# Four layers on one core, attention: the bf16 parts of q and k are made and read back one attention step further ahead

## The reference

```
x = layernorm(x + mamba(x))        # selective scan, 256 channels, 16 states
x = layernorm(x + ffn_fp4(x))      # gate/up/down with blockwise fp4 of x, h and the weights
x = layernorm(x + attention(x))    # the layer that the change touches
x = layernorm(x + mlp(x))          # 128 -> 512 -> 512 -> 128 with weights +1/-1
```

```
q, k = rope(x Wq), rope(x Wk)                    # per map, 8 dimensions
o1   = softmax(q1 k1^T * 8**-0.25) v             # v has 16 columns per head
o2   = softmax(q2 k2^T * 8**-0.25) v
o    = rms_norm(o1 - lam * o2) * ln_w + ln_b ;   out = (o * (1 - 0.8 + 0.6 exp(-3.6))) Wo
```

## Time and profile before

| | us |
|---|---|
| median of 3 runs | 1071.04 |
| lowest and highest run | 1065.42, 1078.87 |
| the profiled execution's own time | 1068.53 |
| its span, first to last instruction | 1066.7 |

### The profile page before, as it was taken

The page is one execution under the profiler, slowest core; times in us unless marked ns, Lnnn a source line. Parts: engine busy times, 40 slices in busy tenths (PEclk is TensorE's granted clock), DMA queues, the critical chain, the costliest instruction groups (busy, mean ns, idle before and its releaser), DMA issues.

```text
span 1066.7 us, 14636 instructions
## 1 busy us (share of the span) xinstructions
PE 912.0 (85%) x4466; PEld 481.7 (45%) x4482; DVE 891.7 (84%) x1337; ACT 731.5 (69%) x1600; POOL 788.1 (74%) x560
## 2 busy tenths in 40 slices
PE   7697979897989797786888679999999898699995
PEld 3233434342434343233556454565655543355453
DVE  4799999999999999998885667787777783479996
ACT  3776868686868686544565457777777768777872
POOL 2798998989898989875777734575756535767773
PEclk9899999899999999899999889999999999899998
DMA  4762535353434434003400323332323210000001
GB/s 149 318 239 79 205 113 200 118 199 119 177 142 152 166 141 177 0 1 81 66 0 16 104 76 90 92 99 83 99 83 102 80 47 2 0 2 12 18 21 30
DMA packets 35168, 104.03 MB, mean 98 GB/s; under 512 B 3659, under 2 KB 22475, under 8 KB 24395
## 3 DMA queue, kind: packets, MB, share of 16 engines
q1 hardware_dynamic: 35095, 103.16, 28.9%
HBM read 93.84 MB, written 8.91 MB: 96 GB/s over the span
## 4 chain that ended last, share of the span: by engine, by line
DVE 28%; PE 26%; issue 17%; ACT 15%; DMA 7%; POOL 4%; SPq 4%; DVEq 1%; POOLq 0%; ACTq 0%
PE bank L1644 11%; DVE bank L333 8%; PE bank L610 8%; DMA ks<-parts 6%; PE bank L2002 4%; DVE m_hC L342 4%; DVE a_nm L1410 3%; ACT bank L461 2%; DVE m_hS L333 2%; ACT L461 2%; SPq L1362 1%; DVE m_du L347 1%; SPq L1373 1%; DVE x_all L122 1%; DVE bank L914 1%
## 5 line engine op out<-in xcount | busy, mean ns | idle before, releaser
L610 PE MATMUL bank<-m_hC,ident 128*128 128x512 f32 x512 | 257.8, 627 | 61.4 <-POOL m_hC L568 22.7
L558 POOL TENSOR_TENSOR m_dBu<-m_du,m_Bt 128x1024 f32<-128x1024 f32 x128 | 299.3, 2356 | 12.6 <-DMA m_Bt<-bcd 11.8
L333 DVE TENSOR_TENSOR_SCAN bank<-bank,m_dBu 128x512 f32<-128x512 f32 x184 | 222.4, 1219 | 16.5 <-ACT bank L461 12.6
L1410 DVE TENSOR_REDUCE a_nm<-bank 128x2 f32<-128x512 f32 x256 | 169.3, 687 | 66.7 <-PE bank L1644 66.5
L1581 ACT ACTIVATE late<-bank 128x512 f32<-128x512 f32 x256 | 148.9, 600 | 65.2 <-PE bank L1644 63.4
L610 PEld LDWEIGHTS bank<-m_hC,ident 128*128 128x128 f32 x512 | 93.9, 196 | 203.9 <-issue 111.5
L461 ACT ACTIVATE bank<-m_delta,early 128x510 f32<-128x510 f32 x256 | 170.0, 677 | 0.3
L1644 PE MATMUL bank<-ks,qs 72*128 72x256 bf16 x512 | 100.4, 279 | 28.7 <-DMA ks<-parts 16.8
L342 DVE TENSOR_TENSOR m_hC<-bank,m_Ct 128x512 f32<-128x512 f32 x184 | 123.3, 670 | 0.0
L568 POOL TENSOR_TENSOR m_hC<-m_hS,m_Ct 128x512 f32<-128x512 f32 x72 | 94.6, 1315 | 26.6 <-DVE m_hS L333 26.6
L458 ACT ACTIVATE bank<-m_zero 128x2 f32<-128x2 f32 x181 | 31.2, 173 | 115.5 <-DVE m_hC L342 114.9
(11 more groups left out here) (217 smaller groups left out, 1797.1 us busy)
## 6 DMA issues: line engine op xcount, KB each, us to landing
m_Bt<-bcd SPq DMA_DIRECT2D x32, 1024.0 KB, 6.3
m_Ct<-bcd SPq DMA_DIRECT2D x32, 1024.0 KB, 6.6
qs<-parts SPq DMA_DIRECT2D x16, 576.0 KB
ks<-parts SPq DMA_DIRECT2D x48, 192.0 KB
parts<-a_part SPq DMA_DIRECT2D x32, 192.0 KB, 2.2
out<-x_all SPq DMA_DIRECT2D x8, 256.0 KB, 2.3
vx<-in_vrow SPq DMA_DIRECT2D x4, 256.0 KB
qs<-in_fill SPq DMA_DIRECT2D x1, 768.0 KB
```

Source lines behind the costliest of these rows:

```text
L333: nc.vector.tensor_tensor_scan(out, decay, dBu[:, g % RD], 0.0, ALU.mult, ALU.add).then_inc(scan_ready, 1)
L558: nc.gpsimd.tensor_tensor(dBu[:, g % RD:g % RD + CH], du[:, n % 2], Bt[:, s].unsqueeze(1).broadcast_to([P, CH, GTOK]), ALU.mult).then_inc( ...
L610: return nc.tensor.matmul(out, lhsT, rhs, start=start, stop=stop)
L1410: nc.vector.tensor_reduce(nm[:, slot % 2, q, 2 * pair:2 * pair + 2], s1[i % 2][:], AX.X, ALU.max, negate=True).then_inc(max_ready, 1)
```

## The change

Everything that was done for item n + 3 in step n's first slots is now done for item n + 4 in step n's last slots, so each item is ready earlier.

- GpSimd: `rotate(n+4)` stays at u = 7 (10 in the lone steps). `normalize(n-3)` moves from u = 0 to u = 8. `residual_high(n+4)` stands at u = 9 (lone: 13), `copy_x(n+5)` at u = 10 (lone: 6), `residual_middle(n+4)` at u = 11 (lone: 15). The wait for the transposes of x moves from `residual_middle` to `copy_x`. `head_norm` stays at u = 14.
- ScalarE: the cast to the high part moves from u = 15 to u = 12, the cast to the middle part from u = 4 of the next step to u = 15 of the same.
- SyncE: in a step the three rows go out first, then the parts of item n + 4 are written and read back, into the slot that item n still uses; the read waits until the scores of item n are done (`s2_ready`).

No instruction is added or taken away.

```diff
     def sync(sp):
         def body(n, slot):
-            m, s = n + 3, (slot + 3) % RING
-            if has(n, 3):
-                sp.wait_ge(split_p, 2 * m + 2)
-                for i in range(2):
-                    sp.dma_start(k.parts[i].rearrange("a p t -> p a t"), part[:, :, i, :]).then_inc(parts_out, 16)
             if has(n, 1):
                 sp.wait_ge(nmT_ready, n + 2)
...
-            if has(n, 3):
+            if has(n, 4):
+                m = n + 4
+                sp.wait_ge(split_p, 2 * m + 2)
+                for i in range(2):
+                    sp.dma_start(k.parts[i].rearrange("a p t -> p a t"), part[:, :, i, :]).then_inc(parts_out, 16)
                 sp.wait_ge(parts_out, 32 * m + 32)
+
+                wait(sp, s2_ready, MAPS * (n + 1))
...
-                sp.dma_start(qs[0:ROWS, s].rearrange("r m t -> r (m t)"),
+                sp.dma_start(qs[0:ROWS, slot].rearrange("r m t -> r (m t)"),
...
-                    sp.dma_start(ks[24 * a:24 * a + 24, s].rearrange("r m t -> r (m t)"), k3).then_inc(q_in, 16)
+                    sp.dma_start(ks[24 * a:24 * a + 24, slot].rearrange("r m t -> r (m t)"), k3).then_inc(q_in, 16)
...
             wait(pool, q_in, 64 * m)
-            wait(pool, x_turned, min_group(m + 2, BATCH))
             nc.gpsimd.tensor_tensor(part[:, 2].rearrange("p a t -> p (a t)"), res[:],
...
             for u in range(MAPS):
-                if u == 0 and has(n, 3):
-                    residual_high(n + 3)
-                if u == 0 and has(n, -3):
+                if u == (6 if lone(n) else 10) and has(n, 5):
+                    wait(pool, x_turned, n + 5)
+                    copy_x(n + 5)
+                if u == (10 if lone(n) else 7) and has(n, 4):
+                    rotate(n + 4)
+                if u == (8 if has(n, 4) else 0) and has(n, -3):
                     normalize(n - 3)
-                if u == 5 and has(n, 3):
-                    residual_middle(n + 3)
-                if u == 6 and has(n, 5):
-                    if not has(n, 3):
-                        wait(pool, x_turned, n + 5)
-                    copy_x(n + 5)
-                if u == 7 and has(n, 4):
-                    rotate(n + 4)
+                if u == (13 if lone(n) else 9) and has(n, 4):
+                    residual_high(n + 4)
+                if u == (15 if lone(n) else 11) and has(n, 4):
+                    residual_middle(n + 4)
                 if u == 14 and has(n, -1):
                     head_norm(n - 1)
...
-                if u == 4 and has(n, 3):
-                    act.wait_ge(split_p, 2 * (n + 3) + 1)
-                    nc.scalar.activation(part[:, 1].rearrange("p a t -> p (a t)"), res[:], ACT.Copy).then_inc(split_a, 1)
...
-                if u == 15 and has(n, -2):
-                    squares(n - 2)
-                if u == 15 and has(n, 4):
+                if u == 12 and has(n, 4):
                     m = n + 4
                     act.wait_ge(rope, 2 * m + 2)
                     wait(act, parts_out, 32 * m)
                     wait(act, split_p, 2 * m)
                     nc.scalar.activation(part[:, 0], rot[:], ACT.Copy).then_inc(split_a, 1)
+                if u == 15 and has(n, -2):
+                    squares(n - 2)
+                if u == 15 and has(n, 4):
+                    act.wait_ge(split_p, 2 * (n + 4) + 1)
+                    nc.scalar.activation(part[:, 1].rearrange("p a t -> p (a t)"), res[:], ACT.Copy).then_inc(split_a, 1)
                 yield
```

## The result

| | before | after |
|---|---|---|
| median of 6 runs each, us | 1071.88 (1065.42 to 1078.87) | 1058.26 (1057.07 to 1059.37) |
| ratio, 95% interval | | 0.987 (0.984 to 0.990) |
| the profiled execution, us | 1068.53 | 1057.07 |
| its span, us | 1066.7 | 1055.2 |

The kernel is 1.3% faster: 13.6 us in the medians, 11.5 us between the two profiled executions, against 16.2 forecast for the latter. The median lies inside the stated range of 1044 to 1064. TensorE is busy for 915 us, 912 before, so the time came out of waits (first row: the page's part 1, which answers to the earlier trace rows; then TensorE's waits: line, releaser, us in total, times, longest).

A forecast was written before the change was run, and what follows sets the result against it. Attention was taken as bound by TensorE's own list, a too-late read and something on VectorE; -11.5 (ten steps), -2.0 (step 12), -4.2 (early steps) and +1.5 (VectorE contact) gave -16.2 us, from 1068.5 to 1052, range 1044 to 1064.

The forecast's parts named there:

- The read in the middle: Steps 1 to 11: parts read lands 6 us before it is wanted, its waits go, -11.5 us over ten steps.
- The contact on VectorE: head_norm beside VectorE's five short instructions: only its last row holds a cast, 0.15 us a step, +1.5 us in all.
- rival 1: GpSimd's head_norm takes over the hold of VectorE in every step: 8.5 us back, 1060 us; chance 0.13.
- ScalarE's second cast: ScalarE's cast to the middle part, before slot 0's exponential: starts 0.8 us after its input, so costs nothing.
- rival 4: ScalarE held at the second cast by a late input: 15 steps grow, 1078 us at 2.5 us late; chance 0.07.
- the sign named for it: ScalarE waiting on GpSimd's `a_res` in front of L1630 would speak for rival 4.
- The small rows: Three rows sent at 8.0 us, queued behind the read: land about 14.5, wanted at 15.9, hidden with 1.4 us cover.
- Step 12 and the tail: Step 12 loses its 1.94 us wait for the read: -2.0 us with the small aftershock.
- The early steps: Steps -4 to 0 beside the fp4 layer, waits of 6.90 and 3.27 us: -4.2 us, bounds 0 and -10.2.

The follow-up runs named there:

- e7: Changed kernel plus one unused GpSimd 128x512 subtraction a step right behind head_norm, over VectorE's short instructions: 1070.73 us, ratio 0.997 to the kernel before.
- e4: Changed kernel with head_norm ahead of residual_high on GpSimd in the steps that make parts: 1092.61 us, ratio 1.017 to the kernel before.
- e3: Kernel before, with SyncE issuing the read of the parts ahead of the three small rows: 1150.28 us, ratio 1.071.
- e9: Changed kernel run once more, unaltered: 1058.57 us, ratio 0.986 to the kernel before.
- e1: Changed kernel with the old order for the first four items (steps -4 to -1): 1061.11 us, ratio 0.987 to the kernel before.
- e2: As e1, but residual_middle at slot 1, second cast at slot 2, and the read ahead of the small rows: 1058.67 us, ratio 0.986 to the kernel before.
- e6: Changed kernel with e2's early order for item 0 (step -4) alone: 1055.90 us, ratio 0.984 to the kernel before.
- e5: Changed kernel with e2's early order for items 0 and 1 (steps -4 and -3) only: 1056.06 us, ratio 0.983 to the kernel before.
- e10: The kernel of e6 run once more, beside e9 on one chip: 1059.25 us, ratio 0.987 to the kernel before.

## Why the prediction was right, and which term was wrong

- **The read in the middle: right.** All five waits of the ten steps went, and the steps take 16.63 us each; 16.5 and 0.15 of contact were forecast. The read was issued 3.2 us into the step, a little behind the 2 to 3 I gave; by the 9.2 us that it took before it lands 6 us ahead of its use.
- **The contact on VectorE: right, and rival 1 excluded.** The cast is held 0.13 us (in step 2 0.36), by `head_norm`'s last row, and the power holds nothing. e7 shows what a full hold would have cost: 0.7 us a step, 7.1 over the ten, to be set beside the 8.5 that rival 1 gave for eleven. By the rule of the Trainium skill (SBUF — State Buffer, section SBUF: two separate sides), that a GpSimd instruction which starts first holds the shared pair for its whole length against VectorE's two-port or two-input instructions, the cast and the difference at 720.01 and 720.22 should have been held by the power. They were not; for the subtraction in e7 the rule holds to 0.1 us.
- **ScalarE's second cast: right, and close.** The reserve is 0.9 us and was worked out as 0.8. e4 used it up and made the kernel 1.7% slower than before, so rival 4 named a true mechanism. From step 0 on this order does not meet it. In steps -4 to -1 it does: there the sign named for it, ScalarE waiting for `a_res` in front of L1630, stands four times, 0.78 us and three times 1.26, about the 1.2 us for the subtraction that the forecast had set down for these steps.
- **The small rows: right.** Their flight doubled, hidden by their slot. e3 shows the price without that cover.
- **Step 12 and the tail:** -2.0 forecast, -1.7 measured, which the spread of that stretch does not resolve.
- **The early steps: the mis-sized term.** The step that failed reads "Followed through step -1, the first exponential comes 1 us earlier; step 0 then loses its 3.27 us. Together -4.2 us." Measured: +1.0 and, in e9, +0.6. The first exponential came 3.7 us later (632.77, before 629.11), and step 1 began at 650.37, not near 645.7. Step by step, in the profile: step -4 +4.0, step -3 -1.2, step -2 -0.1, step -1 0, step 0 -1.7. Three things were missing from my working. First, in step -4 I counted the subtraction and the second cast as 1.8 us ahead of L1056, and overlooked L1017, which now stands behind a cast that waits 4.20 us for `rotate`: TensorE's 4.17. Second, with the 6.90 gone, TensorE stands before the fp4 layer's L1164, which waits for VectorE, and then L1171 for ScalarE. I had taken GpSimd's wait of 1.67 as what arrives; L1171 came 0.63 us earlier. Third, the low clock after the stall lasted longer: from the start of L1171 to the end of L1179 there are 3.36 us (601.63 to 604.99) where there were 1.79 (602.26 to 604.05), 1.6 us more. Step -1 then began 2.15 us later than before, and inside it the second cast with its wait put the first exponential off by another 1.5 us. So in step 0 TensorE no longer waits 3.27 us for the read, but 2.05 us for that exponential, where it had waited 0.55: that leaves the -1.7.

That the waits changed their names is shown by their sum over the stretch, all of TensorE's waits taken together: 22.1 us before, 10.2 of them for the read, and 21.4 after, none of them for the read. Five orders of the early steps (before, changed, e1, e2 and e6) stand at 89.9 to 92.9 us whatever TensorE's waits are called. The kernel before has one profile only, so that whether the changed order loses 1 us there or nothing is not settled; that it does not gain 4.2 is.

In e9 the waits of the stretch are only 18.9 us, yet it takes 91.8: the mean granted clock is 0.87 there, 0.89 in the first profile of the changed kernel and 0.91 before. Behind a stall of 6.9 us (before, e1) L1171 took 1.12 and 1.13 us, behind stalls of 4.0 and of 2.9 with 0.9 us (changed, e6, and both again) 2.07 to 2.08. The length of the stall does not tell it by itself: in e2 and e5, behind waits of 3.20 and 2.85 us, L1171 took 1.12, but the clock fell again at about 612 and 613, and the L1171 of the next step took 2.07 and 2.08. That the low clock is what eats the gain is argued, not shown: I tried no kernel that keeps TensorE busy there, and e2, with the quick L1171, is no shorter than the changed kernel. Open too is whether e5's order is worth its 2 us; it was not run again, and e10 says that a few runs and one profile do not tell.

## What to carry to other kernels

A wait in front of a late transfer is worth its full length only where nothing else paces the stretch: in ten attention steps 4.7 us of waits (the 16.8 less those of steps -2, 0 and 12) gave back 10.25 us, since TensorE's waits for VectorE's maxima went with them, from 5.4 us to 0.4; in the steps beside another layer 10.2 us of waits gave back nothing in the two profiles of the changed kernel. When a piece moves up in an in-order list, look for every instruction of the other layer that it now stands before, not only the one that was looked up. And cut traces at a fixed instruction: the middle stretch repeats to 0.1 us where whole executions differ by 3 or more.

## What the runs showed of the hardware

- GpSimd's power (2.91 us, 128x16) let VectorE's cast and two-input difference pass at 0.17 and 0.19 us; GpSimd's subtraction of 128x512 held the like for 0.97 us, until its own end.
- The three small rows, 8 KB each, landed in 1.8 us ahead of the read, in 3.8 behind a read issued 5 us before, in 5.7 behind one issued 3 us before.
- After a stall of 4.0 us TensorE's granted clock was 0.50 for the whole of 598 to 606 us, and two 128x512 matmuls took 2.08 us instead of 1.13; after the longer stall of 6.90 us in the kernel before it was back at 602. In e1, with that stall, the same matmuls stand so; the second row is e2's, one step on, where the clock fell again at about 611.7 with no wait of TensorE over 0.82 us in the ten us before:

```profile
604.74 1.12 PE L1171 MATMUL bank<-x_all,ident 128*128 128x512 f32 x2 [1.29 <-ACT x_all L1063]
...
617.82 2.07 PE L1171 MATMUL bank<-x_all,ident 128*128 128x512 f32 x2 [1.29 <-ACT x_all L1063]
```
